# A mean-embedding projection on one core: the first mean's chain reordered, and idle matmuls placed at three points of TensorE's order

## What is computed

```python
valid = sequence_ids < emb_table.shape[0]          # (1024, 200), table (12500, 512)
safe_ids = jnp.where(valid, sequence_ids, 0)
seq_emb = emb_table[safe_ids]
seq_emb = seq_emb * valid[..., None].astype(seq_emb.dtype)
denom = jnp.maximum(valid.sum(axis=1, keepdims=True).astype(seq_emb.dtype), 1.0)
user_repr = seq_emb.sum(axis=1) / denom            # (1024, 512)
logits = user_repr @ proj_w + proj_b               # (512, 12500) -> (1024, 12500)
```

## Time and profile before

| | |
|---|---|
| time, three executions | 633.05, 634.0, 633.22 us; median 633.22 |
| profiled execution | 632.95 us, of it the span of the profile 631.1 us |
| PE matmul busy | 607.6 us, 96 % of the span |
| DVE busy | 407.2 us, 65 % |
| POOL busy | 232.2 us, 37 % |
| granted clock of PE | 0.997 mean |

### The profile page before, as it was taken

How to read it: one execution, slowest core, us unless ns; L and a number is a source line. 1 busy time by engine, 2 the same in 40 slices (tenths; PEclk the granted TensorE clock), 3 DMA queues, 4 the chain that set the end, 5 groups by cost and what they waited for, 6 DMA issues and landing times.

```text
span 631.1 us, 7599 instructions
## 1 busy us (share of the span) xinstructions
PE 607.6 (96%) x2604; PEld 477.1 (76%) x2604; DVE 407.2 (65%) x721; ACT 146.2 (23%) x163; POOL 232.2 (37%) x227
## 2 busy tenths in 40 slices
PE   1989999999999999999999999999999999999997
PEld 0337657778788777788888888888888888888886
DVE  7988978889896699598698455433333333343442
ACT  8917425132132131120020023111000112111210
POOL 5777877777574377664475000000000000000000
PEclk9989999999999999999999999999999999999999
DMA  9979999999899589888688349935455555566632
GB/s 307 386 259 341 385 393 399 375 320 292 291 319 327 193 279 321 266 251 284 210 285 316 139 133 309 311 120 176 157 179 180 179 169 173 188 186 212 212 112 98
DMA packets 77703, 158.31 MB, mean 251 GB/s; under 512 B 9287, under 2 KB 65042, under 8 KB 77658
## 3 DMA queue, kind: packets, MB, share of 16 engines
q1 hardware_dynamic: 60378, 110.30, 51.0%
q0 software_dynamic: 17280, 47.47, 22.5%
HBM read 115.70 MB, written 51.20 MB: 264 GB/s over the span
## 4 chain that ended last, share of the span: by engine, by line
PE 89%; DVE 5%; DMA 3%; issue 1%; ACT 0%; POOL 0%; POOLq 0%; DVEq 0%
PE acc L853 82%; PE turned L802 4%; DMA rows<-in_L_rec_emb_table_dram,index 3%; DVE sums L569 1%; PE acc L858 1%; DVE w_lo L633 1%; PE turned L794 1%; PE turned L774 0%; DVE top L522 0%; DVE key L526 0%; DMA ids_sb<-in_r_sequence_ids_dram 0%; DVE count L660 0%; ACT w_hi L430 0%; PE turned L788 0%; POOL rows L361 0%
## 5 line engine op out<-in xcount | busy, mean ns | idle before, releaser
L361 POOL DMA_INDIRECT rows<-in_L_rec_emb_table_dram,index x208 | 222.4, 1069 | 101.9 <-issue 60.8
L853 PE MATMUL acc<-w_hi,mean_hi 128*128 128x500 f32 x800 | 224.1, 402 | 0.8 <-ACT mean_hi L446 0.8
L648 DVE TENSOR_TENSOR stage<-acc,bias_sb 128x500 f32<-128x500 f32 x160 | 107.3, 676 | 173.8 <-PE acc L853 173.2
L853 PE MATMUL acc<-w_hi,mean_lo 128*128 128x500 f32 x800 | 213.6, 388 | 0.7 <-DVE mean_lo L620 0.7
L853 PE MATMUL acc<-w_lo,mean_hi 128*128 128x500 f32 x800 | 214.1, 389 | 0.0
L853 PEld LDWEIGHTS acc<-w_hi,mean_lo 128*128 128x128 f32 x800 | 150.3, 188 | 32.1 <-DVE mean_lo L620 1.2
L853 PEld LDWEIGHTS acc<-w_hi,mean_hi 128*128 128x128 f32 x800 | 150.2, 189 | 32.0 <-issue 4.3
L853 PEld LDWEIGHTS acc<-w_lo,mean_hi 128*128 128x128 f32 x800 | 150.3, 188 | 31.5
L569 DVE SCALAR_TENSOR_TENSOR sums<-rows,mask,sums 128x512 f32<-128x512 f32 x165 | 124.2, 753 | 19.5 <-issue 7.3
L430 ACT ACTIVATE w_hi<-w_raw 128x2000 fp32r<-128x2000 f32 x39 | 72.9, 1876 | 220.1 <-PE acc L853 197.7
L633 DVE TENSOR_TENSOR w_lo<-w_raw,w_hi 128x1000 fp32r<-128x1000 f32 x74 | 85.3, 1195 | 13.1 <-ACT w_hi L430 13.1
(11 more groups left out here) (106 smaller groups left out, 187.9 us busy)
## 6 DMA issues: line engine op xcount, KB each, us to landing
out_dram<-stage SPq DMA_DIRECT2D x200, 250.0 KB, 3.8
w_raw<-in_L_rec_proj_w_dram SPq DMA_DIRECT2D x39, 1000.0 KB, 7.5
bias_sb<-in_L_rec_proj_b_dram SPq DMA_DIRECT2D x39, 250.0 KB, 5.8
raw_at_hi<-in_L_rec_proj_w_dram SPq DMA_DIRECT2D x4, 1000.0 KB, 14.1
rows<-in_L_rec_emb_table_dram,index POOLq DMA_INDIRECT x208, 6.2
raw_at_lo<-in_L_rec_proj_w_dram SPq DMA_DIRECT2D x3, 1000.0 KB, 16.5
stage<-in_L_rec_proj_w_dram SPq DMA_DIRECT2D x1, 1000.0 KB, 26.1
ids_sb<-in_r_sequence_ids_dram SPq DMA_DIRECT2D x1, 700.0 KB, 4.4
```

What stands on the lines that cost most here:

```text
L361: return pool.indirect_dma_start(out=dst, out_offset=None, in_=table, in_offset=bass.IndirectOffsetOnAxis(ap=column, axis=0), bounds_check ...
L648: dve.tensor_tensor(stage[:, g % STAGE, r - stores[g][0]], acc[:, r % BANKS, 0:BW], bias_sb[:, i % BIAS], ALU.add).then_inc(s_moved_by_dve, 1)
L853: last = nc.tensor.matmul(bank, first, second, start=part + k == 0, stop=part == 2 and k == K - 1 and not by_act[r])
```

## The change

Six edits: two numbers move `sum_rest(0)` and `list_rest(1)` four columns up in PE's list (REST_FIRST_AT 18 to 14, LIST_FIRST_AT 21 to 17). On DVE, the scaling of its own share of the first mean moves ahead of `w_low(3)` (`first_further_share`), and three of the five sort rounds of tile 2 move from ahead of `first_mean` to behind `mean_low(0)` (SORTED_FIRST = 2). On PE, `keep_clock` puts matmuls whose result nobody reads into a bank that is free: 4 ahead of `turn(0)` and 3 behind it (bank 4, on `w_hi` of block 0), and 6 between the rest and the columns of tile 1 (bank of unit 9, on `mean_hi` of tile 0).

```diff
+    SORTED_FIRST = 2
     OTHERS_FIRST = 7
-    FURTHER_BEHIND, LIST_FIRST_AT, BIAS_DUE = 20, 21, 3
+    FURTHER_BEHIND, LIST_FIRST_AT, BIAS_DUE = 20, 17, 3
...
-    LATE_LOAD, REST_FIRST_AT, OPENED = 7, 18, SPLIT - 1
+    LATE_LOAD, REST_FIRST_AT, OPENED = 7, 14, SPLIT - 1
...
+            def first_further_share():
+
+                dve.tensor_scalar(mean[:], sums[:], inv_count[:, 0:1], None, ALU.mult).then_inc(s_further_mean, 1)
+
             def first_mean():
 
-                dve.tensor_scalar(mean[:], sums[:], inv_count[:, 0:1], None, ALU.mult).then_inc(s_further_mean, 1)
                 dve.wait_ge(s_further_mean, 1)
...
             sum_further(0)
+            first_further_share()
             w_low(3)
-            for r in range(ROUNDS):
+            for r in range(SORTED_FIRST):
                 sort(2, r)
             first_mean()
             mean_low(0)
+            for r in range(SORTED_FIRST, ROUNDS):
+                sort(2, r)
             for c in range(FAST, FAST + 4):
...
+            def keep_clock(times, bank, held):
+
+                for _ in range(times):
+                    nc.tensor.matmul(acc[:, bank, 0:BW], held[:, 0:P], held, start=True, stop=True)
+
...
+            pe.wait_ge(s_w_lo, OPENED)
+            keep_clock(4, SPLIT - 1, w_hi[:, 0, 0])
             turn(0)
+            keep_clock(3, SPLIT - 1, w_hi[:, 0, 0])
...
+                if r == joined[1] - 2:
+                    wait_moved(pe, r - BANKS)
+                    keep_clock(6, r % BANKS, mean_hi[:, 0, 0:BW])
                 for c in range(FAST, COLS):
```

## The result

The changed kernel is slower: 634.96 us (median of 20 runs, 634.23 to 636.64) against 633.06 us (20 runs, 632.39 to 634.09). The ratio is 1.0032, 95 % interval 1.0026 to 1.0038, so about 2.0 us; the span of the profiled execution grew from 631.1 to 633.1 us. The forecast was 634.5 us. Three of the 20 executions of the changed kernel took 636.5 to 636.6 us, the others at most 635.6; none of the three was profiled, and what lengthened them is open.

A forecast was written before the change was run, and what follows sets the result against it. Bound by PE, with DVE's `mean_of(1)` and column 51's gather about equally late at `turn(1)`. PE's 0.8 us gain is given back, DVE adds 1.3 us: 634.5 us, 8-in-10 range 632.8 to 635.4.

The forecast's parts named there:

- What bounds the kernel: At `turn(1)`: column 51's gather and DVE's `mean_of(1)` about equally late; both must come earlier for a faster kernel.
- The term that decides: DVE's three sort rounds, 2.8 us, now ahead of column 26, make `mean_of(1)` and so `turn(1)` 1.3 us late.
- The sum of PE's side: PE from tile 0's columns to column 51: 0.8 us won at the first unit, all given back ahead of column 51.
- Costed at nothing: Idle matmuls, DVE's early share and half-clock stretch taken as about free; the picking moves only within PE's path.
- Its own signs: New profile: column 51 near 85.1 us, `turn(1)` idle about 1 us; wrong if 1.2 GHz shows after 49 us.
- PE arrives late too: Tile 1's first diagonal late, PE idles 1.6 us, clock falls: about +1.8 us, 635.0 us; chance 0.12.
- the gathers move: DVE ops slide against POOL's beat, stretching gathers by up to 0.94 us each: about 635.1 us; chance 0.05.
- DVE catches up: The 1.30 us idle ahead of column 43 absorbs DVE's delay; time stays 633.2 us; chance 0.18.
- Faster: The 0.8 us won at the first unit carries through `turn(1)`: 632.4 us; chance 0.10.

The follow-up runs named there:

- experiment 4: The 13 idle matmuls alone, added to the kernel before: 633.13 us, ratio 1.0001.
- experiment 5: The two numbers alone (rest ahead of column 14, picking ahead of column 17), on the kernel before: 633.22 us, ratio 1.0002.
- experiment 6: The changed kernel with the first four diagonals of tile 1 three units earlier on ACT: 635.12 us, ratio 1.0027 against the kernel before.
- experiment 2: The kernel before with DVE's part alone (share early, three sort rounds late): 634.97 us, ratio 1.003.
- experiment 9: The kernel before with tile 1's rest and columns behind unit 9, and what hangs on them one unit later: 631.88 us, ratio 0.9981.
- experiment 3: The changed kernel without its 13 idle matmuls: 635.61 us, ratio 1.0038 against the kernel before.
- experiment 1: The changed kernel with all five sort rounds ahead of the first mean again: 633.15 us, ratio 1.001 against the kernel before.
- experiment 8: The changed kernel with four diagonals of tile 1 earlier and the sort of tile 3 behind `mean_of(1)`: 635.38 us, ratio 1.0039 against the kernel before.
- experiment 10: The kernel before with tile 1's columns behind unit 9, plus the seven idle matmuls around `turn(0)`: 631.69 us, ratio 0.9976.
- experiment 11: The kernel before with tile 1's columns behind unit 9, seven idle matmuls, two numbers and early share, five sort rounds first: 631.12 us, ratio 0.9972.
- experiment 7: The changed kernel with the sort of tile 3 moved behind `mean_of(1)`: 635.8 us, ratio 1.0047 against the kernel before.

## Why the prediction was right, and where it was not

**What bounds the kernel** held. Two floors at `turn(1)`, DVE and the last gather, left nothing of what PE won at the first unit. Experiments 4 and 5 give PE's parts alone: no change. Experiment 6 shows PE back at its old time and waiting for DVE.

**The term that decides** had the right sign and mechanism and was too small: +1.3 forecast, +1.93 measured at `mean_of(1)`. Its parts: the three rounds took 51.58 - 48.59 = 2.99 us, not 2.82 (one of the three was stretched to 1.12 us); the first unit and `mean_low(0)` came 0.71 us earlier, not 0.8; the wait for column 29 and the small gap ahead of it gave back 0.49, not 0.7. That is 2.99 - 0.71 - 0.49 = 1.79 us at the end of column 29, and the sort of tile 3 took 0.14 us more. The rest of the way to the 2.0 us of the span lies in the one later wait, 0.89 instead of 0.74 us.

**The sum of PE's side** was right in kind: columns of tile 0 end at 45.72 us (forecast 45.5), unit 0 starts at 48.09 (48.0), DVE idles 2.65 us (some 2), column 26 at 51.58 (51.3). But its working names the wrong source. It credits the 0.9 us to the rest leaving PE's path and takes the half-clock stretch of before as free. In experiment 2 the rest stands in its old place, the clock stayed up, and the columns end at 45.62 us all the same:

```profile
40.99 4.63 PE L809 MATMUL turned<-rows,diags_at_lo 128*128 128x512 f32 x10
```

Experiment 9, also with the rest in its old place, ends them at 45.64 us, and experiments 3 and 5, with the rest moved, at 45.6. In experiments 2 and 5 alike the weight load of column 23 waits for its gather and starts at 42.77 us. So that gather sets the end, as the prediction says, wherever the rest stands; what held the profile of before back by 0.8 us was its stretch at half clock.

**Costed at nothing, rightly:** the idle matmuls and the two numbers (experiments 4 and 5), and the early share, which was run only together with other parts (experiment 1).

**Its own signs** came out mixed. Column 51 was to start near 85.1 us and started at 86.93; the turn was to idle about 1 us and its weight loads idled 0.42. A stretch at 1.2 GHz after 49 us, which it named as a sign that the forecast is wrong, is there. That the time still came out 0.5 us from the forecast is in part luck: the second late path happened to end together with DVE's and so added nothing.

**The rival "PE arrives late too" came true beside the forecast**, not instead of it. The prediction expected the diagonal at 78.0 us, an idle time of 1.6 us and a fall of the clock; the profile has 78.60, 1.87 and 0.57. It weighed the two against each other at 0.55 and 0.12, while in the profiled execution they are one cause with two arms of about equal length. In the profiles of experiments 2 and 3, without the six idle matmuls, this arm was the longer one. The rival's price, up to 1.7 us for the stretch at half clock, is not borne out over all executions: seven of the changed kernel's 20 had a mean clock of 1.000 and took 634.66 us in the median, nine had 0.997 and took 634.82 us.

**The rival "the gathers move" was there as well**, hidden behind the other two: in the changed kernel's profile column 51's gather landed 0.7 us late and held nothing, and in experiment 8 it was 1.7 us late and held PE. The prediction costed it by stretched gathers on POOL. In experiment 8 these made 0.4 us; the greater part was the time to landing, which I had taken for fixed. The prediction also misread one row: the gather at 68.96 us began in the second half of its `w_low` op, which ran from 68.84 to 70.03 us, not in the first, and was held to that half's end.

**"DVE catches up"** is refuted: the idle time behind `sum_further(1)` moved along (1.35 us at 83.40), as did the wait for `w_hi` of block 5. **"Faster"** is refuted by the result, and for PE's parts alone by experiments 4 and 5.

## What to carry to other kernels

Work that is moved from ahead of a wait to behind it is not gone: an engine with a strict list turns the wait into idle time and pays for the work later. Here 0.7 us won at the first mean cost DVE 1.9 us at the second, because DVE had no slack in between. Before shortening a chain, look for the next point at which several engines meet, and count what each of them brings there; if two arrive together, relieving one buys nothing, and delaying what feeds both delays all of them. Where the floor of a stretch is a transfer, the gain lies in giving the waiting engine a unit of its other work (experiments 9 to 11), not in reaching the wait sooner.

## What the runs showed of the hardware

**A gather waits for a DVE op with two inputs in SBUF.** A gather's instruction on POOL that begins inside one half of DVE's `w_low` (one input from `w_raw`, one from `w_hi`, both in SBUF) is held until that half has ended, and takes 0.87 to 0.88 us more. In the changed kernel and in experiment 6 the same two instructions meet in another order. Changed kernel, DVE and then POOL:

```profile
77.83 2.30 DVE L637 TENSOR_TENSOR w_lo<-w_raw,w_hi 128x1000 fp32r<-128x1000 f32 x2
```

```profile
77.92 1.98 POOL L362 DMA_INDIRECT rows<-in_L_rec_emb_table_dram,index  x1 [0.46 <-issue]
```

Experiment 6:

```profile
78.11 2.31 DVE L641 TENSOR_TENSOR w_lo<-w_raw,w_hi 128x1000 fp32r<-128x1000 f32 x2 [0.34 <-ACT w_hi L435]
```

```profile
77.77 1.00 POOL L366 DMA_INDIRECT rows<-in_L_rec_emb_table_dram,index  x1 [0.46 <-issue]
```

Begun 0.09 us behind the op the gather took 1.98 us, begun 0.34 us ahead of it 1.00 us. In the whole trace 22 gathers of the kernel before and 20 of the changed kernel began inside such a half, over 0.15 us ahead of its end; 21 and 19 were held, and the exception in each began only 0.04 us behind the half's start. Where one input lies in PSUM the gather is not held: none of 6 and 6 inside the `w_low` ops that read `acc`, none of 62 and 64 inside the `add_column` ops, which read `sums`, a PSUM tile, too. One of them, inside the op that starts at 37.21 us in the earlier trace rows:

```profile
37.74 1.00 POOL L361 DMA_INDIRECT rows<-in_L_rec_emb_table_dram,index  x1 [0.30 <-issue]
```

The Trainium skill, SBUF — State Buffer, Who interferes with whom, says that a DVE instruction with two SBUF inputs contends with a GpSimd instruction that reads SBUF, but infers that a tensor_tensor leaves descriptor writing alone. These rows (1.98 against 1.00 us) fit the first, since a gather has its row numbers (`index`) in SBUF, and not the inference, as the earlier trace rows did not; the prediction told only the second.

**The clock fell behind every gap of 1.87 us and more, and behind some shorter ones.** In the profiles it fell behind idle times of PE of 1.87, 2.09, 2.41, 2.97 and 3.29 us (the changed kernel, experiments 6, 7, 2 and 3), behind 1.63 us in the profile of before, and in experiment 9 behind 1.53 and 0.78 us. It stayed at 1.00 behind 1.56 and 1.59 us in the place of those 1.63 us (experiments 2 and 4), and in experiment 5 behind 1.46 and 0.78 us. A fall costs what no later wait hides. In the profile of experiment 6 `turn(1)` and part of unit 10 ran at half clock, and from the start of `turn(1)` to that of unit 11 it took 4.72 us instead of 3.25, 1.5 us more. Over many executions the fall hardly shows: of the kernel before, the 12 with a mean clock of 0.997 beside experiments 1 to 4 took 633.24 us in the median, the six with 1.000 took 633.17 us.
